# Tokens in chunks of 256, 512, 512, 512 and 256 in place of four chunks of 512

## The reference

```python
mod = silu(c) @ wmod                       # sa, ca, ga, sb, cb, gb
h = layernorm(x) * (1 + ca) + sa
# scan, for each of 256 features and N = 16 states
x_dbl = h @ x_proj_w.T                     # split: dt (128), B (16), C (16)
delta = softplus(dt @ dt_proj_w.T + dt_proj_b)
h_t = exp(delta_t * A) * h_(t-1) + delta_t * B_t * x_t
y_t = sum over n of h_t[n] * C_t[n] + D * x_t
x = x + ga * y
h = layernorm(x) * (1 + cb) + sb
g, u = (h @ gate_w.T) * gate_s, (h @ up_w.T) * up_s       # 704 wide
x = x + gb * ((silu(g) * u) @ down_w.T) * down_s
```

## Time and profile before

| | us |
|---|---|
| median of 3 runs | 378.87 (378.71 to 379.2) |
| the profiled execution, first to last instruction | 381.0 |
| step -1 (front work of chunk 0, to the first scan) | 35.2 |
| step 0 | 76.5 |
| step 1 | 79.9 |
| step 2 | 78.4 |
| step 3 | 69.6 |
| behind the last scan | 41.4 |
| DVE busy | 316.1 |
| PE busy | 260.1 |
| POOL busy | 207.9 |
| ACT busy | 200.0 |

### The profile page before, as it was taken

How to read it: one execution, slowest core, us unless ns; L and a number is a source line. 1 busy time by engine, 2 the same in 40 slices (tenths; PEclk the granted TensorE clock), 3 DMA queues, 4 the chain that set the end, 5 groups by cost and what they waited for, 6 DMA issues and landing times.

```text
span 381.0 us, 3907 instructions
## 1 busy us (share of the span) xinstructions
PE 260.1 (68%) x1212; PEld 197.4 (52%) x1212; DVE 316.1 (83%) x482; ACT 200.0 (52%) x320; POOL 207.9 (55%) x153
## 2 busy tenths in 40 slices
PE   8934544962652679756595897485779756669996
PEld 8534424552541556545374655373557545447774
DVE  2143999799999988999999899999998998993531
ACT  3431644571552686739535868386455556832610
POOL 2007464936597786465768665676685939321000
PEclk9995566775855569968997899779985968699999
DMA  5059940073040500620304216504022700000101
GB/s 171 3 151 369 235 67 0 3 163 60 19 92 1 110 2 0 174 51 20 92 2 73 37 55 137 89 0 112 1 63 48 158 10 0 0 2 0 55 2 58
DMA packets 15958, 25.57 MB, mean 67 GB/s; under 512 B 1344, under 2 KB 6656, under 8 KB 15936
## 3 DMA queue, kind: packets, MB, share of 16 engines
q1 hardware_dynamic: 15520, 24.48, 26.9%
q10 hardware_dynamic: 416, 0.81, 0.6%
HBM read 23.06 MB, written 2.23 MB: 66 GB/s over the span
## 4 chain that ended last, share of the span: by engine, by line
DVE 46%; PE 26%; issue 16%; ACT 6%; DMA 3%; POOL 1%; DVEq 0%; SPq 0%; ACTq 0%; POOLq 0%
DVE state L873 22%; DVE resid L796 11%; PE stateT L1056 5%; PE side L1003 4%; PE side L939 4%; PE side L1036 4%; DMA wmod_sb<-in_wmod 3%; PE side L1020 3%; DVE u L743 2%; DVE gates L771 2%; PE side L916 2%; PE stateT L900 1%; ACT decay L660 1%; DVE resid L708 1%; PE side L953 1%
## 5 line engine op out<-in xcount | busy, mean ns | idle before, releaser
L507 POOL TENSOR_TENSOR state<-u,brow 128x1024 f32<-128x1024 f32 x64 | 152.0, 2384 | 25.1 <-DMA brow<-bT_dram 25.0
L1056 PE MATMUL stateT<-ident,state 128*128 128x128 f32 x512 | 94.2, 336 | 102.1 <-DVE resid L796 68.2
L1056 PEld LDWEIGHTS stateT<-ident,state 128*128 128x128 f32 x512 | 72.7, 172 | 129.9 <-DVE state L873 116.3
L660 ACT ACTIVATE decay<-delta,A 128x512 f32<-128x512 f32 x128 | 87.0, 690 | 87.4 <-DVE state L873 85.0
L873 DVE TENSOR_TENSOR_SCAN state<-decay,last,state 128x512 f32<-128x512 f32 x96 | 117.4, 1264 | 9.2 <-ACT decay L660 9.1
L796 DVE SCALAR_TENSOR_TENSOR resid<-stateT,C_sb,resid 128x256 f32<-128x256 f32 x192 | 78.3, 469 | 0.0
L478 POOL COPY last<-state 128x2 f32<-128x2 f32 x48 | 10.0, 209 | 64.1 <-DVE state L873 63.8
L873 DVE TENSOR_TENSOR_SCAN state<-decay,state 128x512 f32<-128x512 f32 x32 | 37.1, 1202 | 2.8 <-ACT decay L660 2.8
L488 POOL TENSOR_TENSOR acc<-acc,prod 128x1024 f32<-128x1024 f32 x12 | 28.3, 2361 | 17.9 <-ACT prod L642 17.9
L1003 PE MATMUL side<-h_hi,ffn_hi 128*128 128x512 f32 x88 | 34.8, 479 | 0.6 <-DVE gates L771 0.6
L1003 PE MATMUL side<-h_lo,ffn_hi 128*128 128x512 f32 x88 | 30.8, 435 | 2.5 <-POOL h_lo L367 2.5
(11 more groups left out here) (98 smaller groups left out, 302.4 us busy)
## 6 DMA issues: line engine op xcount, KB each, us to landing
brow<-bT_dram SPq DMA_DIRECT2D x16, 1024.0 KB, 8.3
resid<-in_x SPq DMA_DIRECT2D x4, 512.0 KB, 11.1
out<-resid SPq DMA_DIRECT2D x8, 256.0 KB, 2.2
wmod_sb<-in_wmod ACTq DMA_DIRECT2D x1, 768.0 KB, 6.0
wmod_sb<-in_wmod SPq DMA_DIRECT2D x1, 768.0 KB, 11.6
ffn_sb<-in_gateT SPq DMA_DIRECT2D x1, 640.0 KB, 10.3
ffn_sb<-in_upT SPq DMA_DIRECT2D x1, 640.0 KB, 7.8
down_sb<-in_downT SPq DMA_DIRECT2D x1, 640.0 KB, 8.1
```

What stands on the lines that cost most here:

```text
L507: nc.gpsimd.tensor_tensor(state[j % RING_STATE][:, :, 0:S], u[:, c % 2, :, 0:S], b.unsqueeze(1).to_broadcast([P, HALVES, S]), ALU.mult).th ...
L660: nc.scalar.activation(decay[i % RING_DECAY][:, 0:S], delta[:, c % 2, h, 0:S], ACT.Exp, scale=A[:, h * N + n:h * N + n + 1]).then_inc(deca ...
L1056: ins = nc.tensor.transpose(to[:, b * D + h * P:b * D + (h + 1) * P], of[:, h, (2 * q + b) * P:(2 * q + b + 1) * P], ident[:, :])
```

## The change

The list of chunks gets five entries. Chunks 1 to 3 stay at 512 tokens but begin 256 tokens earlier, and chunks 0 and 4 have 256. There are five steps with scans instead of four, 80 slots instead of 64, and five loads of `x`. The instructions of the two short chunks are the same as those of a long one, over 256 columns or two blocks instead of 512 columns or four blocks. All plans keep their slot numbers.

```diff
-CHUNK = [512, 512, 512, 512]
+CHUNK = [256, 512, 512, 512, 256]
 NCH = len(CHUNK)
 TOK0 = [sum(CHUNK[:c]) for c in range(NCH)]
 NBLK = [s // P for s in CHUNK]
```

## The result

The changed kernel takes 391.87 us (median of four runs, 391.14 to 393.19), the kernel before 378.94 beside it: the ratio is 1.035, with a 95% interval of 1.033 to 1.038. It is slower by 12.9 us, 10.4 more than the forecast and just outside its range.

What follows compares the result with a forecast made beforehand. DVE was taken to bound the scan steps, with waits at both ends. Start 28.0, steps 52.5, 74.7, 77.8, 73.0, 47.8 and tail 29.8 summed to 383.6 us, 381.5 on the median; own range 378 to 385, whole range 371 to 390.

Steps and rivals of the forecast that it cites:

- the anchor: Conversion of the summed time to the median: profiled execution of 381.0 us taken as 2.1 us over the median 378.87.
- step 3: Scans of a 512-token chunk while 256 tokens are prepared: 78.4 to 73.0 us, front work halved less 0.5.
- Start: Time before the first scan: 28.0 us, 7.2 sooner, with 4.8 of it from a brow load of half the bytes.
- rival (c): The brow load costs by its 512 rows and doesn't shrink: first scan at 32.8, median 386.3 us; chance 0.14.
- Step 0: Scans of the first 256 tokens beside front work of a 512-token chunk: 46.8 us work, 5.7 idle, 52.5 together.
- Step 1: Scans of a 512-token chunk with back work of 256 tokens: 79.9 to 74.7 us.
- Step 2: Scans of a 512-token chunk, lacking one output addition of 0.6 us: 77.8 us.
- Step 4: Scans of the last 256 tokens beside back work of a 512-token chunk: 37.8 us work, 10 idle, 47.8 together.
- Tail: Work behind the last scan, paced by PE: 41.4 to 29.8 us, with fewer down products and shorter gate and up products.
- (a): Cover holds: idle time of the two short steps stays at 3.6 and 4.4 us, median 373.8 us; chance 0.30.
- (b): PE becomes the bound of step 4 if its clock falls to 0.5: 56 us there, median 392; chance 0.14.

Runs made afterwards that it cites:

- a_brow: Changed kernel with each load of brow issued as two DMAs of two states, each with its own semaphore: 391.53 us, 1.037 of the kernel before.
- a_wmod: Changed kernel with the second wmod load issued first on SP's queue, ahead of the bT store and first brow load: 390.88 us, 1.031 of the kernel before.
- b_again: The kernel before, unchanged, traced a second time: 379.28 us, span 377.4 us.

## Why the prediction was right or wrong

The direction and the reason were right: the gains at the ends are lost in the steps, to work that moves in, to fixed parts and to idle time. The size was not: 391.87 for 381.5. In spans it is 389.3 for 383.6, so 5.7 us of the 10.4 are in the sum, and 4.7 in the anchor. Three terms failed: the load of brow taken as half (4.3 us), the DVE work of step 3 (3.1), and the 2.1 us taken off the span where 2.6 had to be added (4.7).

- **The anchor.** "The profiled execution took 381.0 us, 2.1 us over the median": 381.0 was the span. In every execution whose time and span are both known the time is 1.8 to 2.4 us over the span (379.28 and 377.4; 391.14 and 389.3), so this one was nearer 4 over the median. And its surplus needn't recur in the changed kernel. I should have read the span against the time, not as the time.
- **Start: 28.0 forecast, 32.3 measured.** The failed step is "I take half the bytes for half the time". The issue came as forecast (16.9, measured 16.65), but the load took as long as with twice the bytes. This is rival (c), to which I gave 0.14, with 32.8. The argument from x, whose rows of 1 KB go at the plain rate, doesn't carry over to a load that writes one DRAM row to all partitions; a_brow shows it costing by the row. The formula that the prediction cites from the Trainium skill (DMA: Bandwidth & Descriptors, "Anatomy of one DMA"), 2.0 us and bytes at 436 GB/s, doesn't fit either: it has 1.2 us less for the half, where the rows have 0.1 less. That section gives it for DMAs that GpSimd issues, and brow is issued by SyncE, which the prediction leaves out. An earlier first scan alone is worth little, though: in a_wmod, of 4.2 us won there 1.0 was left.
- **Step 0: 52.5, measured 53.0, but by two errors that cancel.** The work is 42.6 us and not 46.8: `row_abs` (0.42 us for 2.13), the pair for `u` (2.42 for 4.51) and the cap (1.34 for 1.64) met POOL otherwise and were 4.1 shorter together, which nothing in the prediction foresaw. That the step came out right is luck. The idle time is 10.4 and not 5.7, just past its bound of 10. I had priced slot 4's wait at 3 us if brow kept its 8, and it came, with 2.2. Not foreseen were the waits for PE's transposes, 0.9 us at 58.92 and 1.6 at 78.07; the second stand behind PE's 16 products for the D term, which took 3.6 us. The wait of 3.3 us at slot 8 for ACT is the one that I forecast from the 2.83 of the earlier trace rows.
- **Step 1: 74.7, measured 75.3. Step 2: 77.8, measured 77.9.**
- **Step 3: 73.0, measured 76.1.** "Half of 10.0 less 0.5" fails. The halved front has `u` at 4.55 us as before and the cap at 1.37 for 1.65, since both end about with the POOL instruction that runs beside them, and POOL's were still those of a 512-token chunk. In all, DVE's work is 1.9 us less than in step 2 of b_again, not 4.5. I took every DVE instruction to have 0.13 us fixed and the rest by columns; for scans and additions that held (pairs of 1.26 and 1.38 us, forecast 1.26 and 1.32), for these it didn't.
- **Step 4: 47.8, measured 46.2.** Work 39.3 for 37.8, idle 6.9 for 10. The wait for silu (2.0, and 1.1 for the decay behind it) and that for the decay of slot 4 (1.9) are there, smaller than the 4 and 2.5 that I took.
- **Tail: 29.8, measured 28.5.** Mechanism and terms hold: 24 down products at 0.233 us, the gate and up products at 0.123 (4.90 for 40), the lower bound. I had taken 0.135.
- **Rivals.** (a), cover holds: idle time of the two short steps would have had to be under 13 us together; it was 17.4, and 13.9 and 14.9 where both stand at one end. Nor did it decide the sign: with the 8.0 us of idle time that (a) has, the measured kernel would take 382.5 us (an estimate, 391.9 less 9.4), still over 378.9. (b), PE as the bound: PE is busy 34.4 of 46.2 us in step 4, DVE 39.3, at a granted clock of 0.89; excluded. (c) came true for the load; its other half, a short saving in the tail, did not.
- **The range.** I let it reach 390 for (b), though (b) was priced at 392, and took each other case by itself. What came was three errors that point one way: 4.3 us in the start, 3.1 in step 3 and 4.7 in the anchor, less 1.7 in the rest.

What stays open: how much of the 10.9 us of added idle time another placing of the side tasks over the slots of a short step would win back. No run had other slot numbers for ACT's side work.

## What to carry to other kernels

Before cutting a tile at the ends of a pipeline, count what the cut pushes into the part that is bound: here 8.1 us of the 14.5 won outside was simply moved in, 7.4 were new work, 5.1 of it the fixed parts of the scans, and 10.9 came as waits, most of them because the chain of a long neighbour kept its length while the slots that cover it halved. When a size is halved, ask of each instruction and load what it really costs by: columns, rows, or the length of what runs beside it. And check the span of the one traced execution against the times before summing on it.

## What the runs showed of the hardware

A DVE instruction with two operands in SBUF doesn't end before the POOL instruction that was running when it began. Two for `u` take 0.88 us at the start of the changed kernel's run, with POOL idle, and 4.55 beside POOL's drives. It goes the other way too: where DVE was first, a small POOL copy that takes 0.19 us elsewhere took 3.05, and ended with DVE's instruction, at 52.0:

```profile
48.35 3.59 DVE L851 TENSOR_TENSOR gates<-ffn_hi,ffn_sb 128x2816 f32<-128x2816 f32 x1
48.94 3.05 POOL L478 COPY last<-state 128x2 f32<-128x2 f32 x1
```

The Trainium skill (SBUF — State Buffer, "Who interferes with whom") states the cause: DVE reads its second SBUF operand through a port that it shares with GpSimd, and the lock on the shared ports is exclusive. The traces agree. The cap, which reads one operand, waits as well: it took 1.64 us with POOL's long instructions and 0.68 with short ones. The same section has that for such an instruction only in a mode that uses both ports; no trace here names the mode. The prediction didn't use any of this, and its use is the largest gain of this study: POOL's drive in two instructions costs POOL 11 us more and makes the kernel 2.7% faster.

A load that spreads four rows of DRAM over 128 partitions took 8.4 us for 1 MB and 8.3 for 0.5 MB (medians of the changed kernel's run), and two halves issued back to back landed 5.7 and 9.9 us behind the first issue.
